# Seven block products instead of eight in six of eight batches, operand sums made by DMAs and by VectorE

## The reference, cut to what matters

```
h   = gelu(layernorm(cond) @ w1 + b1);  xw = h @ w2 + b2          # w2: 512 x 8192, 16 MB
x_a, x_b = split(xw) -> (b, 512, 8) each
layer_b = base + x_a @ x_b.T                                       # 512 x 512 per batch
x1 = x + (x + x @ layer_b)
ys = cond / sqrt(512);  d = rsqrt((ys*ys) @ (weight*weight) + eps)
out = x1 + (x1 * ys) @ weight * d
```

## Time and profile before

| | us |
|---|---|
| three timed executions | 330.24, 331.13, 332.84 (median 331.13) |
| the profiled execution's own time | 327.92 |
| its span, first to last instruction | 325.9 |
| its mean granted TensorE clock | 0.992 |

### The profile page before, as it was taken

How to read it: one execution, slowest core, us unless ns; L and a number is a source line. 1 busy time by engine, 2 the same in 40 slices (tenths; PEclk the granted TensorE clock), 3 DMA queues, 4 the chain that set the end, 5 groups by cost and what they waited for, 6 DMA issues and landing times.

```text
span 325.9 us, 3742 instructions
## 1 busy us (share of the span) xinstructions
PE 310.5 (95%) x1466; PEld 240.0 (74%) x1466; DVE 131.6 (40%) x217; ACT 135.5 (42%) x206; POOL 23.9 (7%) x41
## 2 busy tenths in 40 slices
PE   8979987968999899999999999999999999999995
PEld 7845543534688788888888888888888888888883
DVE  2777422111566535434452562714181309231300
ACT  4633313004284636445464374524451436233421
POOL 2460000000041010010010010001000000000000
PEclk9999998999999999999999999999999999999999
DMA  6914779698004146456636645511551156105313
GB/s 199 408 45 143 264 264 361 233 332 333 6 2 129 64 149 206 173 184 193 202 157 205 211 135 189 194 64 64 195 193 64 41 186 226 64 7 189 129 66 129
DMA packets 13441, 53.78 MB, mean 165 GB/s; under 512 B 2016, under 2 KB 2016, under 8 KB 11248
## 3 DMA queue, kind: packets, MB, share of 16 engines
q1 hardware_dynamic: 8816, 36.76, 34.2%
q10 hardware_dynamic: 4608, 16.78, 12.7%
HBM read 36.76 MB, written 16.78 MB: 164 GB/s over the span
## 4 chain that ended last, share of the span: by engine, by line
PE 84%; DMA 10%; DVE 4%; issue 1%; ACT 0%; SPq 0%; DVEq 0%
PE tile L750 54%; PE tile L646 11%; PE aux L673 10%; DMA stream<-in_w2u 8%; PE acc L628 4%; PE aux L663 2%; DMA w1s<-in_w1n 2%; DVE qs L561 1%; PE aux L599 1%; DVE rtmp L443 1%; DVE rtmp L446 1%; PE aux L711 1%; DVE rs L451 0%; DVE lns L493 0%; PE tile L592 0%
## 5 line engine op out<-in xcount | busy, mean ns | idle before, releaser
L750 PE MATMUL tile<-xs,qs 128*128 128x512 f32 x768 | 177.5, 389 | 0.8 <-DVE qs L561 0.8
L750 PEld LDWEIGHTS tile<-xs,qs 128*128 128x128 f32 x768 | 144.1, 188 | 31.1 <-DVE qs L561 1.3
L351 ACT ACTIVATE stream<-tile,dts 128x512 f32<-128x512 f32 x64 | 44.0, 688 | 77.1 <-PE tile L750 77.1
L518 DVE TENSOR_TENSOR xs<-xr,xs 128x1024 fp32r<-128x1024 f32 x32 | 38.9, 1225 | 66.8 <-ACT xs L304 66.2
L646 PE MATMUL tile<-rs,w0s 128*128 128x512 f32 x240 | 59.9, 400 | 0.0
L646 PEld LDWEIGHTS tile<-rs,w0s 128*128 128x128 f32 x240 | 44.4, 190 | 19.1 <-issue 10.1
L261 ACT CAST rs<-rtmp 128x512 fp32r<-128x512 f32 x32 | 19.8, 623 | 47.4 <-PE tile L646 31.1
L451 DVE TENSOR_TENSOR rs<-rtmp,rs 128x512 fp32r<-128x512 f32 x32 | 21.9, 688 | 40.2 <-ACT rs L261 39.9
L304 ACT CAST xs<-xr 128x1024 fp32r<-128x1024 f32 x32 | 33.2, 1050 | 5.1 <-ACT stream L351 5.1
L673 PE MATMUL aux<-rs,w0s 128*128 128x512 f32 x144 | 34.9, 391 | 0.0
L673 PEld LDWEIGHTS aux<-rs,w0s 128*128 128x128 f32 x144 | 26.8, 188 | 6.1 <-DVE rs L451 0.6
(11 more groups left out here) (92 smaller groups left out, 96.1 us busy)
## 6 DMA issues: line engine op xcount, KB each, us to landing
stream<-in_w2u SPq DMA_DIRECT2D x16, 1024.0 KB, 4.8
xr<-in_xT SPq DMA_DIRECT2D x32, 512.0 KB, 3.8
out<-stream ACTq DMA_DIRECT2D x32, 512.0 KB, 2.9
w1s<-in_w1n SPq DMA_DIRECT2D x4, 256.0 KB, 4.5
base<-in_w0T SPq DMA_DIRECT2D x4, 256.0 KB, 6.0
base<-in_wm SPq DMA_DIRECT2D x1, 1024.0 KB, 7.0
base<-in_b2q SPq DMA_DIRECT2D x1, 32.0 KB, 6.8
cond<-in_condT SPq DMA_DIRECT2D x1, 16.0 KB, 1.7
```

Of the source, the lines that this page charges most:

```text
L351: nc.scalar.activation(pairs[:, m % 4, o % 2], tiles[n % BANKS][:], ACT.Copy, scale=dts[:, b, o:o + 1]).then_inc(bank_free, 1)
L518: nc.vector.tensor_tensor(xs[:, h, 1, 2 * cp:2 * cp + 2, :], xr[:, cp], xs[:, h, 0, 2 * cp:2 * cp + 2, :].bitcast(F32), ALU.subtract).then ...
L750: last = nc.tensor.matmul(tiles[n % BANKS][:], qs[:, b % 2, u, cc, cols], xs[:, h, v, cc], start=cc == 0 and (u, v) == (0, 0), stop=cc == ...
```

## The change

1. **Seven products.** x_b is seen as 2 x 2 blocks b11, b21, b12, b22 (512 x 256 each, 128x1024 on chip), Q_b as A11, A12, A21, A22. Batches 1 to 6 (`SEVEN`) take seven block products (Winograd's form of Strassen) of 12 matmuls each; batches 0 and 7 take eight. The order of all 58 products is `PRODUCTS`.
2. **Sums of Q.** S1 to S4 are made on DVE in place (`q_sum`, four 128x512 sums a batch). Seven high and low parts a batch are made, against four 128x512 before (`q_high(k)`, `q_low(k)`), six slots.
3. **Sums of x.** T1, T2 and T4 stand one after the other in one buffer, `chain[b % 2]`: b11 is loaded by SP, then POOL issues a DMA from HBM that adds onto it (`accum_op=ALU.add`, 512 KB), when the `x_low` of the part before is done. T3 is b12 with one such add. Seven high and low parts of 128x1024 a batch, against four, in four slots (`T_SLOTS = 4`).
4. **Where they are made.** `made_at` puts each part `LEAD = 3` products ahead of its use, or later if no slot is free.
5. **Emptying.** Partial sums stay in three pairs of banks; P1, P5, P6, P4 are emptied by ACT, P2, P3, P7 are scaled and added by DVE onto what ACT left (`evict_sum`). P6 adds onto P1's banks, P7 onto P6's, P4 onto P7's, each waiting for the emptying before it. SP issues the stores.
6. **Late weights.** Only batches 0 to 3 go through `base_tiles` (`STORED = 4`). Two chunks of batch 4 are made ahead of the main phase, the other 14 chunks of batches 4 to 7 singly, after products 2, 5, 8, ... 41, in bank aux[0], each copied to a buffer by ACT (`keep_late`). R_5, R_6, R_7 are built at products 6 and 7, 18 and 19, 30 and 31 (`R_AT`).
7. **w2.** Three slots in place of two, and `W2_AFTER` is spread a little differently.

The parts of a batch b (product g of each: P1, P2, P5, P6, P3, P7, P4) are made, by `X_AT` and `Q_AT`, at these products: b11 and b21 at P7 of the batch before, T1 at its P4; b22 and T2 at P2; T3 at P5; T4 at P6. A11 at P3 and A12 at P7 of the batch before, S1 at its P4; S2 at P1, S4 at P2, S3 at P5, A22 at P6.

```diff
-STORED = 5
+STORED = 4
+SLOTS = 5
+STREAMS = 3
+T_SLOTS = 4
+S_SLOTS = 6
+QUARTERS = 6
+LEAD = 3
-W2_AFTER = {(0, 1): 1, (0, 2): 1, (0, 3): 1, (1, 0): 1, (1, 1): 1, (1, 2): 2, (1, 3): 2,
-            (2, 0): 2, (2, 1): 2, (2, 2): 2, (2, 3): 1}
+W2_AFTER = {(0, 1): 1, (0, 2): 1, (0, 3): 1, (1, 0): 2, (1, 1): 1, (1, 2): 2, (1, 3): 1,
+            (2, 0): 2, (2, 1): 1, (2, 2): 2, (2, 3): 2}
+SEVEN = (1, 2, 3, 4, 5, 6)
+WINOGRAD = (("P1", "A11", "b11"), ("P2", "A12", "b21"), ("P5", "S1", "T1"), ("P6", "S2", "T2"),
+            ("P3", "S4", "b22"), ("P7", "S3", "T3"), ("P4", "A22", "T4"))
+WINOGRAD_X = ("b11", "b21", "T1", "b22", "T2", "T3", "T4")
...
+def made_at(order, column, slots):
+    at = []
+    for k, g in enumerate(uses(order, column)):
+        free = uses(order, column)[k - slots][-1] + 1 if k >= slots else -1
+        at.append(max(g[0] - LEAD, free, at[-1] if at else -1, -1))
+    return at
...
+LATE = [(b, cc) for b in range(STORED, B) for cc in range(KC)]
+LATE_AFTER = {2 + 3 * n: LATE[2 + n] for n in range(len(LATE) - 2)}
+R_AT = {}
+for g, (b, cc) in LATE_AFTER.items():
+    if cc == KC - 1 and b + 1 < B:
+        R_AT[g + 1], R_AT[g + 2] = (b + 1, (0, 1)), (b + 1, (2, 3))
...
+        @program.gpsimd
...
+            def add_to_chain(b, n, part, after):
+                pool.wait_ge(x_lo, x_count(b, after))
+                nc.gpsimd.dma_start(chain[:, b % 2], xT[b, part[0], part[1]],
+                                    accum_op=ALU.add).then_inc(chain_added[b % 2], 16)
+            def add_to_b12(b):
+                pool.wait_ge(b12_loaded, 16 * (b + 1))
+                nc.gpsimd.dma_start(xb12[:], xT[b, 1, 1], accum_op=ALU.add).then_inc(b12_added, 16)
...
+        @program.scalar
...
+            def x_high(k):
...
+                    act.wait_ge(chain_added[b % 2], chain_adds(b, ("T1", "T2", "T4").index(part) + 1))
+                    src = chain[:, b % 2]
+                if k >= T_SLOTS:
+                    act.wait_ge(product_done, 2 * (X_LAST[k - T_SLOTS] + 1))
+                nc.scalar.copy(ts[:, k % T_SLOTS, 0], src).then_inc(x_hi, 1)
...
+            for g in range(len(PRODUCTS) + 1):
+                if g > 0 and PRODUCTS[g - 1][1] in ACT_TURN:
+                    evict(g - 1)
+                if g - 1 in LATE_AFTER:
+                    keep_late(*LATE_AFTER[g - 1])
+                for k in range(len(X_ORDER)):
+                    if X_AT[k] == g:
+                        x_high(k)
+                for k in range(len(Q_ORDER)):
+                    if Q_AT[k] == g:
+                        q_high(k)
+                if g in R_AT:
+                    for kc in R_AT[g][1]:
+                        r_high(R_AT[g][0], kc)
...
+        @program.vector
...
+            def evict_sum(g):
+                b, name = PRODUCTS[g][:2]
+                turn, bank, by, o, other = {"P2": (0, 1, dts, 0, "P1"), "P3": (2, 2, ndts, 0, "P6"),
+                                            "P7": (1, 0, ndts, 1, "P5")}[name]
+                at, _ = quarter_of(b, turn)
+                for i in range(2):
+                    dve.wait_ge(product_done, 2 * g + i + 1)
+                    dve.wait_ge(act_out, act_count(b, other, i))
+                    nc.vector.scalar_tensor_tensor(quarter[:, at, i], pairs[(b + bank) % 3][i][:],
+                                                   by[:, b, 2 * o + i:2 * o + i + 1], quarter[:, at, i], ALU.mult,
+                                                   ALU.add).then_inc(dve_out, 1)
...
+            for g in range(len(PRODUCTS) + 1):
+                if g > 0 and PRODUCTS[g - 1][1] in DVE_TURN:
+                    evict_sum(g - 1)
+                for b in range(1, STORED):
+                    if g - 1 in range(FIRST[b - 1], FIRST[b - 1] + KC):
+                        p_sum(b, g - 1 - FIRST[b - 1])
+                for k in range(len(X_ORDER)):
+                    if X_AT[k] == g:
+                        x_low(k)
+                for k in range(len(Q_ORDER)):
+                    if Q_AT[k] == g:
+                        q_sum(k)
+                        q_low(k)
+                if g in R_AT:
+                    b, chunks = R_AT[g]
+                    for kc in chunks:
+                        r_scale(b, kc)
+                    for kc in chunks:
+                        r_low(b, kc)
...
+        @program.tensor
...
+            def product(g):
...
+                    elif name == "P6":
+                        pe.wait_ge(act_out, act_count(b, "P1", i))
+                    elif name == "P3":
+                        pe.wait_ge(act_out, act_count(b, "P5", i))
+                    elif name == "P7":
+                        pe.wait_ge(act_out, act_count(b, "P6", i))
+                    elif name == "P4":
+                        pe.wait_ge(dve_out, dve_count(b, "P7", i))
```

More of the change, by code:

```diff
@@ L191, in _ @@
                 load_w2(unit)
[L192 to L204, removed]
+            load_chain(0)
+            load_b21(0)
+            load_b12(0)
+            load_b22(0)
+            load_chain(1)
+            for g, (b, name, _, _) in enumerate(PRODUCTS):
+                for k in range(len(X_ORDER)):
+                    if X_AT[k] == g - 1 or (g == 0 and X_AT[k] < 0):
+                        owner, part = X_ORDER[k]
+                        if owner + 1 < B and part == "b21":
+                            load_b21(owner + 1)
+                        if owner + 1 < B and part == "b22":
+                            load_b22(owner + 1)
+                        if owner + 1 < B and part == ("T3" if owner in SEVEN else "b12"):
+                            load_b12(owner + 1)
+                        if owner + 2 < B and part == ("T4" if owner in SEVEN else "b11"):
+                            load_chain(owner + 2)
+                if g > 0 and PRODUCTS[g - 1][1] in PLACE:
+                    store(PRODUCTS[g - 1][0], PRODUCTS[g - 1][1])
+            store(PRODUCTS[-1][0], PRODUCTS[-1][1])
+            for i in range(QUARTERS):
+                stores = sum(m % QUARTERS == i for m in range(4 * B)) + (i == (4 * B - 1) % QUARTERS)
+                sp.wait_ge(stored[i], 16 * stores)
+        @program.gpsimd
         def _(pool):
@@ new lines, in _ @@
+            pool.wait_ge(squared, 1)
+            mask_early(0)
+            pool.wait_ge(squared, 2)
+            mask_late(STORED)
+            for g in range(-1, len(PRODUCTS)):
+                for k in range(len(X_ORDER)):
+                    owner, part = X_ORDER[k]
+                    if X_AT[k] == g and owner in SEVEN:
+                        if part == "b11":
+                            add_to_chain(owner, 1, (1, 0), "b11")
+                            add_to_b12(owner)
+                        elif part == "T1":
+                            add_to_chain(owner, 2, (1, 1), "T1")
+                        elif part == "T2":
+                            add_to_chain(owner, 3, (0, 1), "T2")
+                if g in FIRST[:STORED - 1]:
+                    mask_early(FIRST.index(g) + 1)
+                if g >= 0 and g - 1 in LATE_AFTER and LATE_AFTER[g - 1][1] == KC - 1 and LATE_AFTER[g - 1][0] + 1 < B:
+                    mask_late(LATE_AFTER[g - 1][0] + 1)
@@ L261, in r_high, with evacuate_base @@
                 nc.scalar.copy(rs[:, kc, 0], rtmp[:, kc % RTMP]).then_inc(r_hi, 1)
-            def evacuate_base(b, chunks=range(KC)):
-                for cc in chunks:
+            def evacuate_base(b):
+                for cc in range(KC):
                     act.wait_ge(tile_done, b * KC + cc + 1)
@@ L548, in _ @@
             r_low(4, 3)
[L549 to L562 removed]
+            for k in range(2, len(X_ORDER)):
+                if X_AT[k] < 0:
+                    x_low(k)
@@ new lines, in late_chunk, with late_rank @@
+            def late_chunk(bank, b, cc, kc):
+                cols = slice(cc * P, (cc + 1) * P)
+                for u, v in ((0, 0), (0, 1), (1, 0)):
+                    last = nc.tensor.matmul(bank[:], w0s[:, u, kc, cols], rs[:, kc, v],
+                                            start=kc == 0 and (u, v) == (0, 0), stop=False)
+                return last
+            def late_rank(bank, b, cc):
+                pe.wait_ge(late_masked, b - STORED + 1)
+                nc.tensor.matmul(bank[:], amk[:, 1, cc * P:(cc + 1) * P], csq[:, 1], start=False,
+                                 stop=True).then_inc(late_done, 1)
```

495 lines of the change are left out of this document (305 added, 190 removed).

## The result

| | before | after |
|---|---|---|
| median of 4 runs, us | 330.69 (326.62 to 332.84) | 361.27 (359.84 to 362.79) |
| profiled execution's span, us | 325.9 | 360.1 |
| granted clock, mean | 0.992 | 0.953 |
| matmuls | 1466 | 1394 |
| main phase: first product to the end, us | 217.5 | 263.3 |

Executions of one kernel fall into a faster and a slower group, so in this document medians are of all executions and ratios of the faster ones alone. The changed kernel takes 1.0971 of the time of the one before (95% interval 1.0855 to 1.1086). The 34 us of span are the balance of two things. The first product starts at 96.85 us where it started at 108.4, 11.6 us earlier. The main phase behind it is 45.8 us longer, though it has fewer products.

What follows compares the result with a forecast made beforehand. TensorE bounds the kernel before, at 84% of the chain of work. TensorE's gain of 25.3 us, outweighed by 31.7 us of waits in five rounds, gave a span of 332.3; plus 5.2 to the median, 337.5 us (+1.9%), range 310 to 355.

Steps and rivals of the forecast that it cites:

- a serial chain of adds: Main phase: T1, T2, T4 share one buffer, each add waits for the x_low before, so the chain goes round once per batch.
- TensorE's count: Main phase if TensorE alone set it: products, late chunks and rank tiles 201.8 us, plus 3.8 to the end.
- the five rounds: Rounds 2 to 6 of the main phase, one pass of the chain per batch; 31.7 us of waits claimed in them.
- The doubt about the stream's rate: w2 stretch: 372 GB/s needed where a window shows 332, so a rest of 2 us of waits could stay.
- D: Time of one add from x_low to landing: 5.8 us claimed, bounds 3.8 and 7.7.
- cheap adds: Rival, faster: an add lands in 4.8 us or less; at 4.4 the time is 325 us; chance 30%.
- The round, 17.4 + 2D: Once round the chain per batch: 17.4 us of ACT and DVE work plus two adds; decides over TensorE from D = 3.8.
- The slope of 9 us per us of D: Total time moves 9 us per us of D below 5.8, twice a round with batch 4 covering one; 14 above.
- R at bad places: Building late R delays the chain: +3.7 and 3.2 us for batch 6's, +6.1 for batch 7's.
- for batch 0 and 1 TensorE covers them: R's delays in batches 0 and 1, before the waiting rounds, were claimed hidden behind TensorE's work, at no cost.
- one rival only: Rival, POOL held up: D = 7.0, 354 us; repeated waits may lower the clock, 1.5 us each, 7 in all; chance 12%.
- second link: The second add of a round, D + 2.3 us, claimed hidden behind ACT's work up to D = 5.8; waits before P5 or P6 would show it longer.

Runs made afterwards that it cites:

- no_adds: Changed kernel without its 24 accumulating DMAs and the waits for them, x sums left out of the result: 351.62 us, ratio 1.0712.
- no_adds_no_r: Changed kernel without the accumulating DMAs and without building R_5, R_6, R_7: 330.5 us in 10 runs, ratio 0.9856; its trace is of a long execution (333.26 us).
- floor: As no_adds_no_r, with b21 and A12 of the next batch also made one product later: 321.72 us, ratio 0.9747.
- late_b21: Changed kernel with b21 and A12 of the next batch made one product later, at P4 in place of P7: 358.86 us, ratio 1.0847.

## Why the prediction was right or wrong

I forecast 337.5 us, slower by 1.9%, with a range of 310 to 355. It came out at 361.3. The sign holds. The mechanism, a serial chain of adds that sets every round, holds in part: without the adds 45.0 of the 57.7 us over TensorE's count remain. In spans the miss is 360.1 - 332.3 = 27.8 us. By place: the first product 1.8 us later than I had it (96.85 against 95.0), from there to the first of the casts 11.4 more (60.4 against 49.0), the five rounds 9.4 more (167.4 against 158.0), and from the last cast to the end 5.1 more (35.4 against 30.3).

What the main phase costs over TensorE's count, my terms against what the runs took off, in this order:

| over the count of 205.6 | I had | measured |
|---|---|---|
| the adds in the chain | 18.7 | 12.7 (no_adds) |
| R_6 and R_7 in the rounds | 13.0 | 14.7 (no_adds_no_r) |
| R_5, before the rounds | 0 | 7.3 (same) |
| b21 ahead of `evict_sum` of P7 | 0 | 6.1 (floor) |
| rank tiles, masks, other waits, clock | 0 | 16.9 (left in floor) |
| sum | 31.7 | 57.7 |

The two terms that I worked out come to 31.7 against 27.4, partly by luck: the adds were put 6.0 too high. The failure is in what I costed at nothing, 30.3 us. The rows are differences of single traces, so I take each as good to an us or two at best; the 6.1 and the 14.7 rest on the trace of the long execution.

Point by point:

- *Products.* 72 matmuls fewer, as counted. The 16.3 us are real, and are seen nowhere, since TensorE isn't the bound.
- *w2.* 9.2 forecast, 8.7 measured where it stands alone. The doubt about the stream's rate (a rest of 2 us) came true in the changed kernel's staging: 2.3 us of wait in its own trace, base 3 at 74.2 instead of 71.4, and 0 to 4.2 us in the traces that share its head.
- *D.* 5.8 forecast. To landing it is 5.6 in the median, and from the end of `x_low` to the next cast, which is what the round feels, 5.6 to 7.1 in the 14 links where ACT waited, mean 6.2. The Trainium skill's rule (Collectives: The Full Stack, why ReduceScatter is half of AllGather: an add is slower by its second source read), with the formula of DMA: Bandwidth & Descriptors, gave an estimate of 4.4. By the rows of line L397 an add has 5.6 where the plain load from the same queue has 4.1; the rows decide, and the "cheap adds" rival falls by them.
- *The round, 17.4 + 2D.* For the rounds without R it gives 29.0; measured 30.6, 28.1 and 29.95. This is the part that the trace of before could give, and it held within 1.6 us. The slope of 9 us per us of D came near in the sum and not in its parts. For the 1.5 us from 5.6 to 4.1 (plain loads) it promised 13.5 and 12.3 came, but as 3.8, 1.8, 0.8, 0.7 and 5.6 in the five rounds, where my slope is 3.0 for each and 1.5 for the third; that the sum is near is luck. With no adds at all nothing more comes, since TensorE's own program, with its waits, holds a round without R at 27 to 29 in all but the last. I had compared the chain to an average of 25.0 us of TensorE's work. Rounds with three late chunks have 7 x 2.72 + 3 x 2.95 = 27.9, and each has a wait at P4 of up to 3.7 on top.
- *R at bad places.* R_6: 6.9 forecast (3.7 and 3.2, in two rounds), 3.9 and 1.0 measured. R_7: 6.1 forecast, 10.8 measured. I walked ACT and DVE up to T4, and stopped there. What is late next is the late chunk on TensorE that stands ahead of P7 (8.20 us of wait), it then runs at half the clock, and b11's cast comes behind it. **The failed step is "for batch 0 and 1 TensorE covers them"**: R_5 isn't covered. Its chunk (5,0) waits 2.33 us, then takes 5.49 instead of 2.72, and R_5 is worth 7.3 in all, the largest term put at nothing that a run prices by itself. The cover I named was TensorE's work up to the next product; but R's user is a late chunk and stands at once behind it.
- *POOL's masks at nothing.* Wrong: I had them behind the adds and "wanted later than they are ready", and didn't ask how long the add ahead of them waits. These rows of after show it:

```profile
128.47 0.90 POOL L397 DMA_DIRECT2D chain<-in_xT  x1 [6.50 <-DVE ts L727]
...
129.11 2.18 POOL L386 TENSOR_SCALAR amk<-asq,mask 128x512 fp32r<-128x512 f32 x1
...
131.34 0.50 PE L919 MATMUL aux<-csq,amk 128*128 128x512 f32 x1 [2.88 <-POOL amk L386]
```

  The mask was behind an add that waited 6.50 us for `x_low`; it took 2.18 us where 1.56 was usual; TensorE waited 2.88 us for it.
- *Rank tiles.* I had them as 2.7 us of TensorE and no wait. Each needs DVE's `p_sum` of the one before, and DVE does it in its turn behind low parts: 6.4 us of waits in two, 4.2 at 181.3.
- *P4.* I had P7 waiting for P6's emptying and put nothing at P4. It waits for `evict_sum` of P7, two ops that stand behind b11's and b21's low parts (1.22 each). The last part of the kernel shows it, and it covers the 5.1 us there:

```profile
326.73 1.22 DVE L727 TENSOR_TENSOR ts<-chain,ts 128x1024 fp32r<-128x1024 f32 x1
327.86 1.22 DVE L727 TENSOR_TENSOR ts<-xb,ts 128x1024 fp32r<-128x1024 f32 x1
329.00 0.68 DVE L760 TENSOR_TENSOR ss<-base,ss 128x512 fp32r<-128x512 f32 x1
329.60 1.40 DVE L778 SCALAR_TENSOR_TENSOR quarter<-tile,ndts,quarter 128x512 f32<-128x512 f32 x2
...
330.49 10.04 PE L978 MATMUL tile<-ts,ss 128*128 128x512 f32 x36 [3.68 <-DVE quarter L778]
```

  36 matmuls should take 8.2 us, and take 10.04: 3.7 of wait and 1.9 of clock are 5.6.
- *The clock.* I had seen it fall behind waits, and put it into one rival only, 1.5 us each time and 7 in all. My own forecast had five waits of 3 to 8 us in it, so it belonged into the sum. It fell six times, for 34 us, some 12.5 us by the estimate above.
- *The sizes that no row showed.* `evict_sum` takes 0.74 us, I took 0.69.
- *The marks.* w2: not under 1 us but up to 1.3 a wait in the changed kernel, and up to 3.5 in `late_b21`. Adds: 18% of the chain (15% said). TensorE: 42% and not 60%. ACT's casts wait for DMA: yes. "TensorE's waits once a batch, before P7, released by ACT": no. They come before late chunks, rank tiles and P4, released by DVE; ACT had room, DVE's order had not. Two come before P6, 0.46 and 4.30 us, behind the second add: the sign that I had named for a second link longer than my 5.8. That link took 7.1 us in the last round.

Two things stay open. How the 16.9 us left in the floor divide between waits (10.2) and clock (some 5.9) was not separated by a run. That P6 emptied ahead of T4's cast would shorten the round follows from the walk, and wasn't tried.

## What to carry to other kernels

Saving a bound engine's work by giving it to engines that are half idle pays only if their program order has slack, so walk the order of each of them, POOL's too, and for each wait ask what stands behind it and who wants that; this kernel's totals fitted (DVE 56%, ACT 46%) and it still lost 10%. What a bound engine's stall costs is the stall and the slow clock behind it, here 34 us at about half, so a forecast with stalls in it needs the clock as a term. And when a change is a bundle, price each part alone: here the small part (a third slot for the w2 stream, -2.9%) was worth having, the large one was not, and the staging around it seems to have cost what the small part gains. Nor is a link's share of the chain of work its price: the adds had 18% of it, 64 us, and gave 12.7 when they went.

## What the runs showed that I had not expected

- An accumulating DMA of 512 KB from POOL's queue takes 5.3/5.6/6.8 us to landing (minimum, median, maximum), a plain one from the same queue 3.5/4.1/5.6; POOL is busy 0.86 us at its issue against 0.53. The second add, issued right behind the first, takes 10.7 in the median, and POOL 1.21 us at its issue.
- While POOL adds two SBUF tensors (128x1024, 2.7 to 3.2 us), a DVE operation with two sources in SBUF waits for it: up to 2.88 us where it takes 0.69.
- POOL's 512-wide multiplication by a mask, 1.56 us at its shortest, took up to 2.50 us in the changed kernel.
- TensorE's granted clock fell to near its lower level (1.2 GHz) at or behind waits of 2.65 to 8.2 us in the midst of busy stretches, for 3.4 to 10.2 us each time. Behind two waits of 2.2 us, at 148.1 and 162.2 us, it stayed high.
